# A gated state-space block in one kernel: norms summed in 128 rows of 64 steps, state terms by head, and a new order of the work on every engine

## The reference, cut to what matters

```python
bc = jnp.einsum('bti,oi->bto', value, W_bc).reshape(Bsz, Tlen, H, 4, N)
bc = bc / (jnp.sqrt(jnp.sum(bc * bc, axis=-1, keepdims=True)) + EPS)
Bz, Bx, Cz, Cx = (bc[..., 0, :], bc[..., 1, :], bc[..., 2, :], bc[..., 3, :])
...
S = 1.0 / (1.0 + dt_t[..., None] * k_t[..., None] + (dt_t * dt_t)[..., None] * A)
z = S[..., None] * (z - dtE * A[None, :, :, None] * s + dtE * (Bz_t[..., None] * u_t[:, :, None, :]))
s = s + dtE * z + dtE * (Bx_t[..., None] * u_t[:, :, None, :])
y = jnp.einsum('bhn,bhnd->bhd', Cz_t, z) + jnp.einsum('bhn,bhnd->bhd', Cx_t, s)
```

## Time and profile before

| | us |
|---|---|
| median of three runs | 2736.1 |
| the profiled execution's own time | 2735.51 |
| span in its trace | 2733.8 |
| PE busy (share of the span) | 2264.5 (83%) |
| DVE busy | 1873.4 (69%) |
| ACT busy | 1164.3 (43%) |
| mean granted PE clock | 0.843 of 2.4 GHz |
| one evacuation on ACT, L812 and L814 (599 and 598 ns) | 1.2 |

### The profile page before, as it was taken

How to read it: one execution, slowest core, us unless ns; L and a number is a source line. 1 busy time by engine, 2 the same in 40 slices (tenths; PEclk the granted TensorE clock), 3 DMA queues, 4 the chain that set the end, 5 groups by cost and what they waited for, 6 DMA issues and landing times. The chain is left out here.

```text
span 2733.8 us, 56799 instructions
## 1 busy us (share of the span) xinstructions
PE 2264.5 (83%) x20514; PEld 1409.3 (52%) x20514; DVE 1873.4 (69%) x4268; ACT 1164.3 (43%) x2659; POOL 360.2 (13%) x540
## 2 busy tenths in 40 slices
PE   5766478898989898988989898989898997646886
PEld 2333225555555555554555555555555556635775
DVE  5776258776768677767777695867767776537765
ACT  3554225253544445352625354443525352203544
POOL 0000111111111111111111110111111110033210
PEclk9888788898989889988989898988888895557997
DMA  3554533434344343434443444434343433052410
GB/s 99 174 171 152 154 104 89 130 97 110 103 117 116 92 127 98 110 100 115 109 113 93 120 105 105 129 101 108 91 119 104 110 90 77 5 200 108 146 63 23
DMA packets 240312, 299.22 MB, mean 109 GB/s; under 512 B 127904, under 2 KB 144288, under 8 KB 231840
## 3 DMA queue, kind: packets, MB, share of 16 engines
q1 hardware_dynamic: 126688, 144.19, 17.7%
q10 hardware_dynamic: 95808, 113.56, 15.5%
q0 software_dynamic: 17536, 37.78, 5.1%
HBM read 240.85 MB, written 51.39 MB: 107 GB/s over the span
## 5 line engine op out<-in xcount | busy, mean ns | idle before, releaser
L642 PE MATMUL m_ps_a<-m_valT,m_w_bc 128*128 128x512 f32 x2048 | 1062.7, 672 | 68.9 <-DMA m_valT<-scratch_valT 35.5
L642 PEld LDWEIGHTS m_ps_a<-m_valT,m_w_bc 128*128 128x128 f32 x2048 | 426.8, 218 | 576.6 <-issue 566.7
L597 POOL DMA_DIRECT2D m_shear<-scratch_shear x512 | 277.1, 542 | 1800.8 <-DVE m_psi L1004 1609.2
L1000 DVE TENSOR_TENSOR m_prod<-m_psi,m_shear 128x128 f32<-128x128 f32 x1024 | 294.9, 288 | 36.5 <-ACT m_shear L771 11.7
L1004 DVE TENSOR_TENSOR m_psi<-m_psi,m_prod 128x128 f32<-128x128 f32 x1024 | 293.6, 287 | 17.2
L812 ACT ACTIVATE m_sq<-m_ps_a 128x512 f32<-128x512 f32 x256 | 153.2, 599 | 303.5 <-PE m_ps_a L642 237.0
L771 ACT ACTIVATE m_shear<-m_shear,m_A 128x64 f32<-128x64 f32 x512 | 135.8, 337 | 330.9 <-DMA m_shear<-scratch_shear 299.9
L698 PE MATMUL m_ps_g<-m_raw 32*64 32x64 f32 x8192 | 184.9, 249 | 73.0 <-DVE m_g L1108 59.2
L678 PEld LDWEIGHTS m_ps_k<-m_u,m_kT 64*128 64x128 f32 x1792 | 189.6, 196 | 68.0 <-ACT m_kT L838 42.4
L723 PE MATMUL m_ps_k<-m_raw,m_Xb 128*112 128x64 f32 x1024 | 177.0, 306 | 56.8 <-ACT m_Xb L856 56.8
L698 PEld LDWEIGHTS m_ps_g<-m_raw 32*64 32x64 f32 x8192 | 164.4, 159 | 100.2 <-issue 84.4
(11 more groups left out here) (146 smaller groups left out, 2897.7 us busy)
## 6 DMA issues: line engine op xcount, KB each, us to landing
m_scale<-scratch_norm SPq DMA_DIRECT2D x512, 128.0 KB, 3.2
m_w_bc<-in_w_bcT ACTq DMA_DIRECT2D x252, 256.0 KB, 3.0
m_shear<-scratch_shear POOLq DMA_DIRECT2D x512, 64.0 KB, 2.7
m_det<-scratch_ab ACTq DMA_DIRECT2D x64, 256.0 KB, 5.6
scratch_gateT<-gate SPq DMA_DIRECT2D x8, 1024.0 KB, 3.9
scratch_valT<-val SPq DMA_DIRECT2D x8, 1024.0 KB, 4.4
scratch_svgT<-svg SPq DMA_DIRECT2D x8, 1024.0 KB, 5.6
scratch_u<-p_u SPq DMA_DIRECT2D x8, 1024.0 KB, 7.6
```

The costliest lines, as they stand in the source:

```text
L597: pool.dma_start(shear[h * N:(h + 1) * N, w % 2].rearrange("p k g t -> p k (g t)"), spread(src)).then_inc(into.sem, into.step)
L642: mm = pe.matmul(ps_a[j % 2].ap(), w_bc[:, j, kt, :], valT[:, kt, :], start=(kt == 0), stop=(kt == KI - 1))
L1000: dve.tensor_tensor(prod.ap().rearrange("p k g r -> p (k g) r"), psi_kt[of_half][:, :, t, :], window.unsqueeze(2).to_broadcast([P, 2 * HAL ...
```

## The change

Letters below: "first" is the first group of a half row, "then" the first of the next one.

1. **Norms.** `of_segment` holds, for each of 8 segments of 64 steps, the head sums placed so that segment s of head h lands in row 8h+s. `sum_squares` is now 32 matmuls of 32 x 64 that accumulate into 64 columns of `ps_s`. ACT's square root goes straight into `compact`; `rows_`, its four transfers and `compact_in` are gone. `compact` now has one buffer for the whole chain: the root for group g waits until `compact` of g-1 is stored (`rows_stored`).
2. **State terms** by head: 56 matmuls with 32 weight columns and 16 moving columns; `copy_terms` is 4 activations of all 128 partitions in place of 8 of 32.
3. **Shear** is scaled by DVE (`scale_window`, one 128 x 256 operation a window, 12 of 16 steps into the window before), no longer by ACT.
4. **Transfers**: `valT` and `e_end` move from ACT's queue to SP's, `ab` to POOL's; `y` is stored by one transfer a group in place of four and loaded by four in place of one.
5. **Orders**: five units of lead instead of four; PE does one unit before the transposes and one after, cuts the unit that goes with the scores in two halves, one behind each pair of heads, and does one unit between outputs and the next scores. DVE takes two `queries` before the states; the new half row's first `keys` come after the last mask; `det_logs` are done in the half row before.

```diff
-    LEAD, PHASE = 4, UNITS // 2
+    LEAD, PHASE = 5, UNITS // 2
...
+                def norm_rows(b, group):
+                    sp.wait_ge(rows_ready.sem, rows_ready.at(b, group - 1))
+                    load_factor(b + group // HG, group % HG)
+                def input_scales(b, group):
+                    sp.wait_ge(rows_ready.sem, rows_ready.at(b, group))
+                    sp.dma_start(dram["norm"][group % 2].rearrange("r (s t) -> (r s) t", t=SEG),
+                                 compact.ap()).then_inc(rows_stored.sem, rows_stored.step)
+                    sp.wait_ge(rows_stored.sem, rows_stored.at(b, group))
+                    sp.wait_ge(c_scaled.sem, c_scaled.at(b, group - 1))
+                    load_scales(group % 2, 0)
...
+                            if w == NW and not (last and half):
+                                pool.wait_ge(det_used.sem, det_used.at(b, half))
+                                load_ab(b, half + 1)
...
-                    for j in range(NJ):
-                        mm = pe.matmul(ps_s[j * N:(j + 1) * N, :], head_sum.ap(), sq[:, j, :],
-                                       start=True, stop=True, skip_group_check=True)
+                    for s in range(N // HP):
+                        for j in range(NJ):
+                            mm = pe.matmul(ps_s[j * N:(j + 1) * N, 0:SEG], of_segment[:, s, :], sq[:, j, s * SEG:(s + 1) * SEG],
+                                           start=(s == 0), stop=(s == N // HP - 1), skip_group_check=True)
...
+                                for h in range(HP):
+                                    col = (tile * 2 + p_) * DH
+                                    mm = pe.matmul(ps_k[odd][h * N:(h + 1) * N, col:col + DH],
+                                                   kT[rows, p_, tile * P + h * N:tile * P + (h + 1) * N],
+                                                   u[rows, s, tile, h * DH:(h + 1) * DH], start=True, stop=True,
+                                                   skip_group_check=True)
...
-                    product(b, unit, last)
+                        product(b, unit, last, pair * 2, pair * 2 + 2)
...
                         for i in range(HALF):
+                            products(b, unit, 1, last)
                             transposes(b, first + i)
-                            products(b, unit, 1, last)
+                            products(b, unit + 1, 1, last)
                             state_terms(b, first + i)
...
                     act.wait_ge(sums_made.sem, sums_made.at(b, group))
-                    act.wait_ge(compact_in.sem, compact_in.at(b, group * NJ - 1))
-                    act.activation(rows_.ap(), ps_s.ap(), ACT.Sqrt).then_inc(norm_ready.sem, norm_ready.step)
+                    act.wait_ge(rows_stored.sem, rows_stored.at(b, group - 1))
+                    act.activation(compact.ap(), ps_s[:, 0:SEG], ACT.Sqrt).then_inc(norm_ready.sem, norm_ready.step)
...
+                def scale_window(b, half, w):
+                    into = shear_in[w % 2]
+                    dve.wait_ge(into.sem, into.at(b, ((half * NW + w) // 2 + 1) * HP - 1))
+                    v = shear[:, w % 2, 0].rearrange("p (g c) t -> p g (c t)", g=HALF)
+                    of_groups = A[:, half % 2 * HALF:half % 2 * HALF + HALF].unsqueeze(2)
+                    dve.tensor_tensor(v, v, of_groups.to_broadcast([P, HALF, NC * W]),
+                                      ALU.mult).then_inc(steps.sem, steps.one())
```

More of the change, by code:

```diff
@@ new lines, in output_scales @@
+                def output_scales(b, group):
+                    sp.wait_ge(b_scaled.sem, b_scaled.at(b, group))
+                    load_scales(group % 2, 1)
+                load_valT(0)
+                load_e_end(0, 0)
+                for group in range(HALF):
+                    norm_rows(0, group)
+                    input_scales(0, group)
+                    output_scales(0, group)
+                def body(b, last):
+                    for half in range(2):
+                        more = not (last and half)
+                        first = half * HALF
+                        then = first + HALF
+                        if more:
+                            norm_rows(b, then)
+                            input_scales(b, then)
+                            load_e_end(b, half + 1)
+                            output_scales(b, then)
+                            norm_rows(b, then + 1)
+                            input_scales(b, then + 1)
+                            output_scales(b, then + 1)
+                            norm_rows(b, then + 2)
+                        if half == 0 and not last:
+                            sp.wait_ge(a_made.sem, a_made.at(b, UNITS - 1))
+                            load_valT(b + 1)
+                        if more:
+                            input_scales(b, then + 2)
+                            output_scales(b, then + 2)
+                            norm_rows(b, then + 3)
+                        if more:
+                            input_scales(b, then + 3)
+                            output_scales(b, then + 3)
@@ L590, in _, with load_ab @@
             def _(pool):
+                def load_ab(b, half):
+                    for h in range(HP):
+                        first = h * HG + half % 2 * HALF
+                        pool.dma_start(det[h * N:(h + 1) * N, :, :],
+                                       spread(dram["ab"][b + half // 2, first:first + HALF])).then_inc(ab_in.sem, ab_in.step)
                 def load_shear(b, half, w):
@@ L775, in load_valT @@
-                def load_valT(b):
-                    for kt in range(KI):
-                        act.dma_start(valT[:, kt, :], dram["valT"][b, :, kt, :]).then_inc(val_in[kt].sem, val_in[kt].step)
-                def load_ab(b, half):
-                    for h in range(HP):
-                        first = h * HG + half % 2 * HALF
-                        act.dma_start(det[h * N:(h + 1) * N, :, :],
-                                       spread(dram["ab"][b + half // 2, first:first + HALF])).then_inc(ab_in.sem, ab_in.step)
@@ L807, in evacuate @@
                     act.wait_ge(a_made.sem, a_made.at(b, unit))
-                    if unit == UNITS - 1 and not last:
-                        load_valT(b + 1)
                     if j == 0 and unit:
@@ L824, in det_logs @@
                     for i in range(HALF):
-                        group = half * HALF + i
+                        group = half % 2 * HALF + i
                         ins = act.activation(det[:, i, :], det[:, i, :], ACT.Ln, bias=one[:, :], scale=A[:, group:group + 1])
@@ L895, in evacuated @@
                                 unit += 1
-                        def window(w):
-                            hh = half + 1 + w // NW
-                            if not (last and hh > 1):
-                                scale_shear(b, hh, w % NW)
-                        def finish(i):
-                            store_y(b, first + i)
-                            if more:
-                                load_u(b, first + HALF + i)
-                            if i < HALF - 1:
-                                block_states(b, first + i + 1)
+                        evacuated(1)
                         copy_kT(b, first)
                         evacuated(1)
-                        window(2)
                         copy_terms(b, first)
-                        det_logs(b, half)
                         evacuated(1)
@@ L928, in body @@
                         copy_terms(b, first + 3)
-                        if more:
-                            load_e_end(b, half + 1)
-                        window(5)
                         evacuated(2)
@@ L1292, in ffn @@
         x_in = [sig(f"x_in{s}", 1, 16) for s in range(2)]
-        y_in = [sig(f"y_in{s}", 3, 16) for s in range(2)]
+        y_in = [sig(f"y_in{s}", KI + 2, 16) for s in range(2)]
         gated = sig("gated", 1)
```

233 lines of the change are left out of this document (99 added, 134 removed).

## The result

| | before | after |
|---|---|---|
| median of the runs, us | 2734.1 | 2659.5 (2655.3 to 2663.6) |
| ratio, 95% interval | | 0.9726, 0.9695 to 0.9757 |
| profiled execution / its span, us | 2735.5 / 2733.8 | 2660.5 / 2658.8 |
| marker to marker, mean of 15, us | 125.7 | 121.8 |

(The median before takes in a fourth run, of 2727.4 us.) The kernel is 75 us faster where 250 were forecast, and outside the range (2385 to 2610). The forecast was 390 + 15 x 112 + 93 + 324. The same four terms of the profile after, from the timeline (start, length, us) of the marker operations and of the last matmuls (before: the earlier trace rows), follow. The marker is the first multiply of the *second* `keys` of a half row in both kernels; the prediction calls it the first `keys`, which changes neither the period nor its sum.

What follows compares the result with a forecast made beforehand. Waits that PE and DVE hand each other were taken to bound the half row. Start 390 + 15 periods x 112 + last half row 93 + tail 324 = 2487, stated as 2485 us; range 2385 to 2610.

Steps and rivals of the forecast that it cites:

- What bounds the half row: Steady half row of 126.3 us: PE busy 112.8, DVE 93.0, neither full; set by waits the two hand each other.
- The last load of scales ... also ends before mask 3: Mask stretches: the last load of scales, 6.8 us behind the factors, was to end before mask 3.
- DVE's 33 us fit below these 42: Mask 0 to mask 3: DVE's 33 us of work were to fit within the 42 us between these masks.
- The transfers' wait is gone: DVE's 276 us wait for the norms' transfers goes; a group's sums and root are done units before DVE asks.
- The norm hold, 4.5 us a half row: ACT's third-group root waits for `compact`'s store, delaying DVE's states 4.5 us; root waits in over one group of four would refute.
- Rival D: Waits move but stay: the root waits for the store in every group; period near 122, 2637 us; chance 0.04.
- The start, 390: Marker at 390 us instead of 413.8: first factors at 323, each next group's 15.2 later; 24 us saved.
- PE's terms: State terms 1.7 us at 15 ns a matmul, sums 1.0 us; PE's half-row sum falls by 5 to 96 us.
- Rivals C (25 ns): At 25 ns a matmul, state terms give 1.2 us more each, sums 0.6; period 113, 2505 us; chance small, 0.05.
- E: Narrow matmuls of state terms and sums don't overlap, 105 ns each; period 166, 3300 us, slower; chance 0.04.
- rival B: PE stays at the slow clock in the mask loop; period 119.5, 2600 us; chance 0.20.
- The last half row: Without units, at the low clock: 93 us instead of 112, 19 us saved, groups 8.7 to 9 us each.

Runs made afterwards that it cites:

- early, one buffer: Run early with one buffer of `compact` again, so ACT's root waits for the store of the group before; 2563.2 us, ratio 0.9379.
- early: Changed kernel with two `compact` buffers, masks 2 and 3 ahead of the scalings, factors one operation earlier with SP's part; 2503.5 us, ratio 0.9168.
- compact twice: Changed kernel with two buffers for `compact`, so ACT's root waits for the store two groups before; 2588.1 us, ratio 0.9483.
- states back: Changed kernel with only the state terms undone: 28 wide matmuls a group and eight smaller copies on ACT; 2677.9 us, ratio 0.9820.
- `ab` late: Changed kernel with POOL's load of `ab` also waiting for the third coming group's input scaling, ACT's logarithms at half row's end; 2668.7 us, ratio 0.9743.

## Why the prediction was wrong, point by point

- **What bounds the half row** (waits that PE and DVE hand on): right.
- **"The last load of scales ... also ends before mask 3"**: this step failed, and with it the mask stretches. It priced one load, at 6.8 us, measured in the quiet start, and looked at the last one only. In DVE's order the third group's input scaling stands ahead of mask 2; its scales take 14 us with the moved `ab` beside them, 9.7 without. Before, DVE had 11.6 us of its own work (mean) between the store of that group's norms and their use; the new order leaves 7.7, less than the transfers take. The fourth group's scales come 7.9 us behind their factors, near the price, but only 2.8 us of DVE's work stand in between, so mask 3 waits as well. That "DVE's 33 us fit below these 42" compared sums; the waits come from the order inside them. These two stretches lose 8.9 us a period, 134 of the 147 us. The version that repairs the order and keeps the hold (early, one buffer) has 14.4, 15.0 and 13.2 us between its masks, 42.6 where 42.5 were forecast: those terms were right but for the late scales. Its 3 to 0 is 72.6 us where 69.5 were forecast, its period 115.0 by the markers where 112 was; so the repair gives back 95 us and not 134, and why 3 to 0 is 3 us longer is not shown. (Early, without the hold, has a period of 111 to 112; the forecast less its 4.5 us for the hold would be 107.5.)
- **"The transfers' wait is gone"**: right, and it was booked to the whole change. The old transfers are hidden as well, all but 36 us; this I could have looked for in the new order.
- **The norm hold, 4.5 us a half row**: right in size (compact twice shortens the period by 4.6, of which 3.0 in the stretch where I had put it), wrong in how often: the root waits 31 times, for the third and the fourth group of each half row, and I had said that more than one in four would refute me. Rival D had the mechanism and the wrong place: no wait of DVE for the root is left but the first. That its period of 122 is the measured 121.8 is luck.
- **The start, 390**: failed by 32 us. The step is "each next one is four units and a sum behind, 15.2": DVE's own chain of steps and two transfers takes 24.4 us. Spreading the steps brought 23 to 27 us of it back.
- **PE's terms**: state terms of 1.7 us are 1.13, sums of 1.0 us are 1.10:

```profile
1294.67 1.10 PE L678 MATMUL m_ps_s<-m_sq,m_of_segment 128*32 128x64 f32 x64
1295.70 1.13 PE L731 MATMUL m_ps_k<-m_u,m_kT 64*32 64x16 f32 x112
```

  10 ns each for the state terms, where the nearest row had 15. Rivals C (25 ns) and E fall. "TensorE: Matmul & The Clock Gate" of the Trainium skill, section "Wait — 56ns, not 53.3ns?", says that two matmuls never start less than about 25 ns apart; an estimate by it is 2.8 us for the state terms, and the measured 1.13 us decides against it here. In the steady half row the narrow form is hidden, as states back shows.
- **The clock** (rival B): 28 us a half row at 1.2 GHz in the kernel after (mean of 14), 33 before, 18 in early; the mean granted clock is 0.88, where I had written 0.93. Rival B was right that most of the low time stays. That it follows the waits of PE and does not make them is argued from these runs, not tested.
- **The last half row**: 79.7 us instead of 93, better by 13; state terms undone cost 19 us there.
- **The tail**: 331.7 us instead of 324; it was 329 to 336 in every later version. 3.3 us of it lie at its start: the first matmul of `ffn` starts 29.5 us behind the end of `mix` instead of 26.2. It needs a product of POOL that waits for a load (`svg`) queued behind those of `y`, which are now four. No run undoes them, and the rest of the difference stays open.
- **The range**: 2385 to 2610 came from rivals that varied the price of the hold, of the clock and of the matmuls. None was that the moved transfer and the shortened distance make a load late, though the distance was to be read from the order.

## What to carry to other kernels

When an order is changed, work out for every transfer the distance in its consumer's queue between the operation that releases it and the one that waits, in the new order, and set it against the transfer's time under load, store included; the first row of a quiet start is the low end of that time. A buffer that takes the place of a copy ties its writer to its last reader: price the direct form against the copy in the *new* order, where the copy may be hidden. What stands in a queue behind a waiting operation (a mask, an evacuation) pays for it, so independent work goes ahead of the wait, in measured portions.

## What the runs showed of the hardware

- 112 matmuls of 64 rows, 32 weight columns and 16 moving columns, over four groups of columns of the array, take 1.13 us, 10 ns each; 64 of 128 rows with 32 weight columns and 64 moving columns take 1.10 us, 17 ns each.
- A broadcast load of 4 x 128 KB takes 4.8 to 6.7 us (means by its place, in the changed kernel and with `ab` late) with the kernel's usual traffic and 10.8 us beside one of 4 x 256 KB; the store of 32 KB ahead of it lands after 1.5 us for the first group of all, and in the loop after 3.0 us for the third group and 2.1 to 2.2 for the others.
